# A tile's 16 context reciprocals, taken on GpSimd as a power of minus one instead of on VectorE

## The reference, cut to what matters

```
x = x + 0.5 * ffn(layernorm(x))      # job "b" of the kernel
x = x + attn(layernorm(x))           # 16 heads of 16; of each row only the top 31 scores count
x = x + 0.5 * ffn(layernorm(x))      # job "a", same weights
```

```
scores = Q K^T / sqrt(16)                      # 512 x 512
thresh = the 31st largest score of the row
attn   = softmax(where(scores < thresh, -inf, scores))
context = attn V ;  out = context Wo^T + bo
```

## Time and profile before

| | before |
|---|---|
| median of 3 runs | 4729.98 us |
| profiled execution, whole | 4728.35 us |
| its span (first to last instruction) | 4726.4 us |
| VectorE busy | 4394.2 us, 93% |
| TensorE busy (matmuls) | 4139.5 us, 88% |
| ScalarE busy | 3969.8 us, 84% |
| GpSimd busy | 2995.1 us, 63% |
| `crec` on VectorE | 64 reciprocals, 15.0 us |
| `ctxn` on GpSimd | 62 products, 38.8 us |

### The profile page before, as it was taken

How to read it: one execution, slowest core, us unless ns; L and a number is a source line. 1 busy time by engine, 2 the same in 40 slices (tenths; PEclk the granted TensorE clock), 3 DMA queues, 4 the chain that set the end, 5 groups by cost and what they waited for, 6 DMA issues and landing times. The chain is left out here.

```text
span 4726.4 us, 123904 instructions
## 1 busy us (share of the span) xinstructions
PE 4139.5 (88%) x33100; PEld 3430.8 (73%) x33100; DVE 4394.2 (93%) x10203; ACT 3969.8 (84%) x10181; POOL 2995.1 (63%) x4946
## 2 busy tenths in 40 slices
PE   6778899899899989999988998899899999987777
PEld 5556777777777777777777777777777777765556
DVE  2499999999999999999999999999999999999982
ACT  2488889899889988889988998899888899888772
POOL 1445677677667766766776776767667777654440
PEclk8888999999999999999999999999999999998888
DMA  3111111111111111111111111111111111110011
GB/s 99 46 27 35 50 51 54 48 55 50 52 51 50 54 49 54 50 54 51 51 53 50 53 50 51 54 49 55 49 53 51 50 53 50 54 38 26 21 30 50
DMA packets 244185, 232.90 MB, mean 49 GB/s; under 512 B 27123, under 2 KB 176628, under 8 KB 243316
## 3 DMA queue, kind: packets, MB, share of 16 engines
q1 hardware_dynamic: 243444, 224.49, 16.5%
HBM read 214.98 MB, written 9.44 MB: 47 GB/s over the span
## 5 line engine op out<-in xcount | busy, mean ns | idle before, releaser
L1027 DVE MAX8 M<-W 128x8 f32<-128x512 f32 x2688 | 1735.6, 681 | 56.0
L679 PE MATMUL pQ<-wf_sb,HS 128*128 128x192 f32 x8192 | 1548.1, 346 | 83.8 <-POOL HS L419 58.1
L679 PEld LDWEIGHTS pQ<-wf_sb,HS 128*128 128x128 f32 x8192 | 1441.1, 203 | 129.3 <-issue 67.2
L1029 DVE MATCH_REPLACE8 W<-M,W 128x512 f32<-128x512 f32 x1664 | 1115.3, 676 | 0.0
L1072 POOL TENSOR_TENSOR XL<-S,LM 128x512 f32<-128x512 f32 x384 | 445.5, 1160 | 913.9 <-ACT LM L909 895.3
L698 PE MATMUL pST<-ident,S 128*128 128x128 f32 x4096 | 749.2, 283 | 13.3 <-ACT S L897 13.3
L924 ACT ACTIVATE OUT<-S,M 128x512 bf16<-128x512 f32 x1024 | 741.7, 724 | 1.1 <-issue 1.1
L928 ACT ACTIVATE S<-S,M 128x512 f32<-128x512 f32 x1024 | 737.1, 720 | 0.0
L700 PE MATMUL pST<-steep,OUT 128*128 128x128 bf16 x4096 | 732.7, 222 | 0.0
L1029 DVE MATCH_REPLACE8 W<-M,S 128x512 f32<-128x512 f32 x1024 | 684.5, 676 | 0.0
L1027 DVE MAX8 M<-S 128x8 f32<-128x512 f32 x1024 | 651.7, 678 | 29.5 <-issue 17.5
(11 more groups left out here) (267 smaller groups left out, 6590.0 us busy)
## 6 DMA issues: line engine op xcount, KB each, us to landing
RB<-rows_b SPq DMA_DIRECT2D x384, 256.0 KB, 3.2
RB<-rows_a SPq DMA_DIRECT2D x384, 256.0 KB, 3.3
x_b<-in_x SPq DMA_DIRECT2D x64, 128.0 KB, 2.8
out_y<-y SPq DMA_DIRECT2D x64, 128.0 KB, 1.8
wf_sb<-in_wf SPq DMA_DIRECT2D x4, 768.0 KB, 7.4
rows_b<-rwT_b SPq DMA_DIRECT2D x64, 8.0 KB, 1.3
wof_sb<-in_wof SPq DMA_DIRECT2D x1, 1024.0 KB, 7.1
rows_a<-rwT_a SPq DMA_DIRECT2D x64, 8.0 KB, 1.4
```

Of the source, the lines that this page charges most:

```text
L679: mm = nc.tensor.matmul(pQ[:, 0:QKV], HS[:, k % 2, e, i, :], wf_sb[:, i, at:at + QKV], start=k + e + i == 0, stop=(k, e, i) == (3, 3, 1))
L1027: nc.vector.max(m, src[i]).then_inc(s_tk, 1)
L1029: nc.vector.match_replace(W[:, i, :], m, src[i], -BIG).then_inc(s_tk, 1)
```

## The change

The step `ctx_rec` leaves VectorE's own `ffn` function and goes into `layer`, right ahead of `ctx_norm`. Its slot in the table stays 69. So GpSimd now does it for 62 tiles, as a `TENSOR_TENSOR` with the power as operation: sums to the power of -1.0. The last two tiles stay on VectorE with `reciprocal`.

```
@@ layer @@
+            if at := mine("ctx_rec"):
+                t, c = at
+                sums = ctxr[:, c % 2, :, :].rearrange("p g (h e) -> p g h e", h=HG)[:, :, :, HD]
+                held(eng, s_o, GROUPS * t + GROUPS)
+                if ends:
+                    nc.vector.reciprocal(crec[:], sums).then_inc(q["ctx_rec"], 1)
+                else:
+                    nc.gpsimd.tensor_tensor(crec[:], sums, minus_one[:].rearrange("p (g h) -> p g h", g=GROUPS),
+                                            ALU.pow).then_inc(q["ctx_rec"], 1)
             if at := mine("ctx_norm"):
@@ VectorE's ffn @@
-                if at := tile(J, "ctx_rec", w, j):
-                    t, c = at
-                    held(dve, s_o, GROUPS * t + GROUPS)
-                    nc.vector.reciprocal(crec[:], ctxr[:, c % 2, :, :].rearrange("p g (h e) -> p g h e", h=HG)[:, :, :, HD]
-                                         ).then_inc(q["ctx_rec"], 1)
                 if at := tile(J, "top", w, j):
```

## The result

The changed kernel took 4846.2 us at the median of four runs (4841.5 to 4849.0), the kernel before 4730.3 us beside it. The ratio is 1.0245, with a 95% interval of 1.0234 to 1.0257: 116 us slower. Forecast were 4758 us and a range up to 4777 us. The sign was right, the size was off by a factor of nearly four. The profiled execution took 4844.1 us, its span is 4842.2 us.

A forecast was written before the change was run, and what follows sets the result against it. VectorE was taken as the bound. Stalls of 5.5 us a round, 33 us over six rounds, less 3 us saved, gave net +30 us on 4728.35 us: 4758 us, range 4722 to 4777 us.

The forecast's parts named there:

- VectorE is the bound, and pairs in the timeline decide: VectorE, 93% busy, hardly waits; where producer end and reader start lie close, a delay goes straight to it.
- The saving: VectorE's queue: 62 reciprocals removed free 0.09 us each, 5.6 us, of which about 3 us was kept.
- The price of the power: GpSimd: each 128x16 power takes 2.93 us, from the row of `simr`; 182 us for 62.
- the prediction's 0.47 us: GpSimd: the power's cost by the skill's rule of twice VectorE's time; the sum would then hold no stall.
- The path: The power in front of job "a"'s `mixT` delays TensorE's L624, then ACT's scores and `Sr_a`, then VectorE's `mxr_a`.
- TensorE is late by 2.93 - 0.65 = 2.28 us: L624, tile at 2606 us: power's delay less cover, not made up by busy TensorE; VectorE stands 2.0 us.
- The cover of 0.65 us at L624: Tile at 2606 us: L624 started 0.80 us after `mixT` ended; beyond the shortest hand-over, 0.65 us hides delay.
- Three stalls in eight tiles, the others covered by 2.6 to 3.1 us: Per loop round, `mxr_a` stalls 2.0 + 2.1 + 1.4 = 5.5 us; 33 us over six rounds; other tiles left out.
- `nm_b` as one item in a rival: In "More gets through": `nm_b` stands behind the power on GpSimd too, and ACT needs it; no separate size.
- The delay does not pile up: Some 8 us after `mxr_a`, ACT waits for VectorE, 3.95 us in one tile, so lateness ends within each tile.
- More gets through: Rival: small stalls left out, tiles outside the loop, lost saving and `nm_b` give 4771 to 4780 us; chance 0.15.
- The cases with a cheap power: Rivals: power of 0.57 to about 1 us, 4723 us, chance 0.15; with full 235 ns saved, 4714 us, chance 0.08.

The follow-up runs named there:

- The fillers: The changed kernel with six more matmuls on TensorE before the wait for `mixT` in three tiles of four, result overwritten: 4794.3 us, 1.0138.
- Slots 65 and 71: The changed kernel with `ctx_rec` at slot 65 in place of 69: 4750.7 us, 1.0047; at slot 71: 4737.8 us, 1.0013.
- extra4: The kernel before, reciprocal kept, plus an unread GpSimd power of 4 columns at the changed kernel's place: 4736.2 us, 1.0011.
- extra8: The kernel before, reciprocal kept, plus an unread GpSimd power of 8 columns at the changed kernel's place: 4755.7 us, 1.0057.
- extra12: The kernel before, reciprocal kept, plus an unread GpSimd power of 12 columns at the changed kernel's place: 4788.1 us, 1.0126.
- extra16: The kernel before, reciprocal kept, plus an unread GpSimd power of 16 columns at the changed kernel's place: 4842.3 us, 1.0238.
- copy16: The changed kernel with a plain GpSimd copy of the 16 sums in place of the power, division left out: 4726.4 us, 0.9992.

## Why the prediction was wrong in size

- **VectorE is the bound, and pairs in the timeline decide.** Right. All of the loss is VectorE's idle time.
- **The saving.** Right. 0.09 us for each reciprocal was forecast, 0.11 measured, and the run with a copy gained about 4 us, though its interval reaches no change.
- **The price of the power.** Right: 2.93 forecast, 2.94 measured. GPSIMD Engine Reference in the Trainium skill, section Engine selection, puts GpSimd at about twice VectorE's time for an elementwise add, multiply or maximum of two inputs. Carried over to a power, that was the prediction's 0.47 us, and the traces do not bear it out: 2942 ns against the 235 ns of VectorE's reciprocal is 12.5 times. A sentence of Perfetto Trace Analysis in the same skill, section Optimizing GPSIMD Operations, fits this case better: "Prefer implementations on other engines where possible."
- **The path.** `mixT`, then L624, then the scores, then `Sr_a`, then `mxr_a`. Right, each wait of it is in the page or the views of the kernel after.
- **"TensorE is late by 2.93 - 0.65 = 2.28 us".** This is the step that failed. It priced a wait of TensorE at its own length. In the trace after, the wait is 4.4 us in the tile shown, and the rows behind it ran at the granted clock of 0.50 and took 2.5 us more. The rows of the kernel before could have warned: in the tile that was read, 16 `pQ` behind the wait for `rw_b` took 4.54 us and 16 others 2.77 us. The prediction read TensorE only from L624 on. The fillers showed what the missing term was worth: at least 51 us.
- **The cover of 0.65 us at L624.** Wrong in kind. The gap between `mixT` and L624 came at least in part from TensorE being slow earlier in the tile: without that slow stretch the wait for `mixT` grew from 16 to 51 us. Where the slow stretch moved, this cover went: waits of about 3 us behind a power of 1.68 us.
- **Three stalls in eight tiles, the others covered by 2.6 to 3.1 us.** Wrong as a consequence. A cover of 2.9 us hides a delay of 2.3. It doesn't hide 2.3 + 2.5 = 4.8 us. `mxr_a` waited 56 times, in some 60 tiles. With TensorE kept busy it was 29, for 43 us, which is the size that the prediction gave this wait.
- **`nm_b` as one item in a rival.** ACT waited for it 42 times and 55 us in all after the change. Every one of its waits over 0.3 us, 40 of them, was followed within 6 us by idle time of ACT at least as long, mostly for the scores, as in the tile shown. So in the changed kernel this wait was covered, and the rival's item had little to add. With the fillers that holds for 24 of 39 such waits, so there it may cost some microseconds. Slots 65 and 71 free `nm_b` and `mixT` together, and no run freed one alone.
- **"The delay does not pile up".** Neither shown nor refuted. ACT's wait for VectorE's `M`, which was to absorb the delay, fell from 139.8 to 77.5 us over the steady part, so some room was left in it, and still `mxr_a` waited in nearly every tile. That each tile's new delay came before the last had gone is possible, no run tests it.
- **The rivals.** "More gets through" had the right sign and listed 4771 to 4780 us, with a chance of 0.15. None of its items is the one that came. No rival had a term for slow matmuls behind a wait. The cases with a cheap power fell with the first row of the trace after. That the range ended at 4777 us came from the same omission: every bound in it was built from delays that keep their length.

Left open: why the wait for `rw_b`, which is as long after as before (130 and 128 us), is followed by slow `pQ` less often once TensorE also waits at `mixT` (46 of 512 groups over 3.5 us in place of 71). Open too is the exact split of the 116 us: the fillers give 51 us as the least for the slow rows, not their whole share. The runs show that the slow stretches move, not what decides where.

## What to carry to other kernels

Before you put work on an engine with idle time, ask what stands behind it in its queue, not how busy it is: the same 182 us cost 116, 22 or 6 us at three places of one table, and the nearly free place is the one whose reader had started several microseconds after its input was ready. When a delay will make TensorE stand still, do not price it at its own length only. Look in the trace of before for a wait of that size, compare the duration of the matmuls behind it with the same matmuls elsewhere, and add the difference if those matmuls lead to the bound.

## What the runs showed of the hardware

- A power of -1 on GpSimd takes 1.05, 1.68, 2.31 and 2.94 us for 4, 8, 12 and 16 columns of 128 rows, 0.16 us for each column, against 0.235 us for VectorE's reciprocal of 16 columns and 0.20 us for a copy of 16 columns on GpSimd (runs extra4, extra8, extra12, extra16 and copy16).
- A wait of TensorE can cost more than itself. After 4.3 us in which it did nothing, the granted clock went from 1.00 to 0.50, and matmuls that take 1.89 us took 3.75. Adding useless matmuls in such a wait made the kernel 51 us faster. TensorE: Matmul & The Clock Gate of the Trainium skill, section HAM oscillation, tells of a kernel in which a wait brings the clock down in every round of its loop. This trace agrees as to the fall: 1.00 before the wait of 4.3 us, 0.50 behind it. What the runs add is that the place matters: 46 slow groups of `pQ` fewer brought back about 4 us, 34 slow groups of `pFa` fewer brought back 51.
- The slow stretches are not a fixed loss of each wait. With 8 columns the slow rows moved from `pFb` and `pQ` to `pFa`, the sum of the rows behind `mixT` stayed at 311 us, and only 27 us were lost.
